# Attention key parts of heads 2 to 7 repeated into partitions 64 to 127 by DMA from SP's queue instead of by ScalarE and VectorE

## The chip, the core and the metric

The kernel runs on one core of a Trainium2 chip. It is written against the engines directly: TensorE (PE), VectorE (DVE), ScalarE (ACT), GpSimd (POOL) and SyncE (SP), each with its own instruction stream, ordered among each other by semaphores only. The metric is the device time of one execution in microseconds (us), as the median of several executions.

## The reference, cut to what matters

A small vision transformer: a token embedding from sines and cosines, one attention block with relative positions and a feed-forward layer, then a second block with a global norm and a mixture of experts. The change lies in the first attention, which for 4 images of 513 tokens, width 192, 8 heads of 64 channels computes

```
q = (h1 @ wq).reshape(b, l, H, DK)
k = (h1 @ wk).reshape(b, l, H, DK)
bias = (qr + uk + vr) * scale
scores = jnp.einsum('bihd,bjhd->bhij', q, k) * scale + bias
attn = jax.nn.softmax(scores, axis=-1)
out = jnp.einsum('bhij,bjhd->bihd', attn, v)
```

## The kernel before, in words

Scores are wanted at more than the precision of one reduced-precision product, so q and k are each held as a first part and a rest. `q` has the first part of a head in partitions 0 to 63 and its rest in partitions 64 to 127. `kh` has the key's first part, `kl` its rest, each of them in both halves of the partitions, so that one product over 128 partitions with `kh` and one with `kl` give all four combinations (`score`, L692).

The products of an image are the list `PRODS` (L512): 13 products n = 0 to 12, two heads to a product. Products 0 to 3 (`EARLY`) are made during the image before, 4 to 12 at the start of the image. Product 3 is the key of heads 0 and 1; 8, 10 and 12 are the keys of heads 2/3, 4/5 and 6/7; 7, 9 and 11 the queries of the same heads. For each, `take` on ACT copies the first part out of PSUM (L811), and `take` on DVE subtracts it from PSUM to get the rest (L937). `repeat` on ACT then copies `kh` from partitions 0 to 63 into 64 to 127 (L820), and `repeat` on DVE does the same for `kl` (L954). ACT's `repeat` of product n stands in its stream after its `take` of product n+1, the last one (product 12) after the exponential of tile 0. DVE's stands right after its own `take`, the last one after tile 2's `add_bias`. PSUM is shared out in four pairs of banks by a list written out by hand (`late_pair`, L518): a product waits until the product that had its pair was taken.

After the products, the image's 40 tiles g (8 heads times 5 tiles of 112 or 65 query rows) go round one loop. On PE each step has `score(g)` (L692), `flip(g-3)` (transposes, L705) and `position(g+10)` (L674), ten tiles ahead. `position_out` copies the position product into the ring `pos` of RT = 4 buffers, by ACT (L832) or, for every second tile from tile 5 on, by DVE (L963); it waits until the transfer that reads the buffer's former content is done. `add_bias` (DVE, L973) makes the scores with their bias and its ring `bias` has MR = 5 buffers. ACT's exponential is L845, DVE's reciprocal L988, POOL's product L616, and `put` copies the transposed probabilities out (ACT L840, DVE L983).

SP issues all DMAs, in this order for each step g: the store of position tile g from `pos` to the DRAM tensor `shear` (L571), then the load of the skewed bias tile g-4 (L582), which waits for its store and for `add_bias` of tile g-9. So SP's program is one list in which each instruction waits for those ahead of it. Position tiles 0 to 9 are made between the products, tile 10 after `score(0)`.

Of the kernel before, what the change touches and what calls it, by code (L numbers as in the profile page):

```python
# [11 lines left out]
F32 = mybir.dt.float32  # L12
# [13 lines left out]
PADL = L + 1  # L26
# [9 lines left out]
H1, DK1, DV1, NPOS = 8, 64, 24, 32  # L36
# [27 lines left out]
def stand_alone(eng, passed):  # L64


    eng.sem_inc(passed, 1)
# [402 lines left out]
def attention_phase(nc, s):  # L470
# [8 lines left out]
    AHEAD = 10  # L479
# [16 lines left out]
    sem = lambda n: s.sem(f"a_{n}")  # L496
# [4 lines left out]
    (pos_done, pos_out_a, pos_out_d, scores_done, biased, exp_done, flipped, put_a, put_d) = (  # L501
        sem("pos_done"), sem("pos_out_a"), sem("pos_out_d"), sem("scores_done"), sem("biased"), sem("exp_done"),
        sem("flipped"), sem("put_a"), sem("put_d"))
    passed, cls_kept = sem("passed"), sem("cls_kept")
    stored, bias_in = [sem(f"stored{i}") for i in range(RING)], [sem(f"bias_in{i}") for i in range(MR)]
    (total_inv, weighed, values_done, values_out, wo_done, image_done, pad_set) = (
        sem("total_inv"), sem("weighed"), sem("values_done"), sem("values_out"), sem("wo_done"), sem("image_done"),
# [4 lines left out]
    PRODS = [("p", 0), ("p", 1), ("q", 0), ("k", 0), ("v", (0, 1)), ("v", (2, 3)), ("v", (4,))] + [  # L512
        (k, p) for p in range(1, H1 // 2) for k in "qk"]
# [6 lines left out]

    after_product = lambda n, w: [g for g in [2 * (n - EARLY) + w - 2] if 0 <= g < AHEAD]
    NP = len(PRODS)
    first_parts = lambda n: sum({"v": 0, "p": 1}.get(kind, 2) for kind, _ in PRODS[:n])
    NHI = first_parts(NP)
    with ExitStack() as ctx:
# [6 lines left out]
        kh, kl = sb("kh", [128, H1, PADL + 2], F32R), sb("kl", [128, H1, PADL + 2], F32R)  # L532
# [15 lines left out]
        @block.sync  # L548
        def _(sp):
            def stack(i, hg):  # L550

                sp.wait_ge(part3, i * 2 + hg + 1)
                for j in range(G4):
                    for part in range(3):
                        sp.dma_start(qpos[NPOS * part:NPOS * part + NPOS, hg * G4 + j, :],
                                     parts[NPOS * j:NPOS * j + NPOS, hg, part, :]).then_inc(stacked[hg], 16)

            def image(b, more):
                for g in range(NG + LAG):
                    if g < NG:  # L560
                        i0, r = TILES[g % NT]
                        x = g % RING

                        if g >= RING:
                            sp.wait_ge(bias_in[(g - RING) % MR], 16 * (b * (NG // MR) + (g - RING) // MR + 1))
                            stand_alone(sp, passed)
                        if by_vector(g):
                            sp.wait_ge(pos_out_d, b * vector_parts(NG) + vector_parts(g + 1))
                        else:
                            sp.wait_ge(pos_out_a, b * scalar_parts(NG) + scalar_parts(g + 1))  # L570
                        sp.dma_start(s.shear[x, 0:r, L - 1 - REACH:L - 1 - REACH + PADL],  # L571
                                     pos[0:r, g % RT, :]).then_inc(stored[x], 16)
                    if g >= LAG:
                        h = g - LAG
                        i0, r = TILES[h % NT]
                        x = h % RING
                        sp.wait_ge(stored[x], 16 * (b * (NG // RING) + h // RING + 1))
                        stand_alone(sp, passed)
                        if h >= MR:
                            sp.wait_ge(biased, b * NG + (h - MR) + 1)  # L580
                        row = s.shear.rearrange("x r c -> x (r c)")[x, L - 1 - i0:L - 1 - i0 + r * (s.PITCH - 1)]
                        sp.dma_start(bias[0:r, h % MR, 0:L],  # L582
                                     row.rearrange("(r c) -> r c", r=r)[:, 0:L]).then_inc(bias_in[h % MR], 16)
                if more:
                    stack(b + 1, 0)
                    stack(b + 1, 1)
                sp.wait_ge(biased, (b + 1) * NG)
                stand_alone(sp, passed)

            stack(0, 0)  # L590
            stack(0, 1)
            with sp.Fori(0, B - 1) as b:
                image(b, True)
            image(B - 1, False)

        @block.gpsimd
# [31 lines left out]
        def _(pe):  # L628
# [20 lines left out]
            def image(b, more):  # L649
# [10 lines left out]
                def position(g):  # L660
                    h, t = divmod(g, NT)
                    i0, r = TILES[t]
                    if g == 0:
                        pe.wait_ge(prod_free, b * NP + EARLY)
                    else:
                        wait_position_out(g)
                    if g == AHEAD:
                        pe.wait_ge(prod_free, b * NP + last_late(NP, 2) + 1)
                    if g == 0:
# [8 lines left out]
                def score(g):  # L678
                    h, t = divmod(g, NT)
                    i0, r = TILES[t]  # L680
                    if g < 2:
                        pe.wait_ge(prod_free, b * NP + last_late(NP, score_pair(g)) + 1)
                    if t == 0:
                        pe.wait_ge(repeated_h, b * H1 + h + 1)
                        pe.wait_ge(repeated_l, b * H1 + h + 1)
                    if last_in_pair[g] is not None:
                        pe.wait_ge(biased, b * NG + last_in_pair[g] + 1)
                    if g == SUMMING[-1] + 2:
                        pe.wait_ge(values_out, b * 4 + 2)
                    for w in range(2):  # L690
                        for k in (kh, kl):
                            mm = pe.matmul(pairs[score_pair(g)][w][0:r, 0:HALF + 1], q[:, h, i0:i0 + r],  # L692
                                           k[:, h, w * HALF:w * HALF + HALF + 1], start=k is kh, stop=k is kl)
                    mm.then_inc(scores_done, 1)

                def flip(g):
                    i0, r = TILES[g % NT]
                    pe.wait_ge(weighed, b * NG + g + 1)
                    if g == 0:
                        pe.wait_ge(prod_free, (b + 1) * NP)  # L700
                    if g >= 1:
# [30 lines left out]
                def late_product(n):  # L732
# [7 lines left out]
                    else:  # L740
                        pe.wait_ge(prod_free, b * NP + last_late(n, late_pair(n)) + 1)

# [16 lines left out]
                for g in range(NG):  # L759
                    score(g)  # L760
                    if g >= LATE:
                        flip(g - LATE)
                    if g + AHEAD < NG:
                        position(g + AHEAD)
                    if g in SUMMING:
                        for n in range(2 * (g - SUMMING[0]), 2 * (g - SUMMING[0]) + 2):
                            values(0, n // NT, n % NT, G4 * NT, SUMMING[0] - 2)
                    for w in range(2):
                        if more and g - w in EARLY_TILES:
                            early_product(EARLY_TILES[g - w], w)  # L770
# [24 lines left out]
        def _(act):  # L795
# [17 lines left out]
            def repeat(i, n):  # L813

                kind, p = PRODS[n]
                if kind == "k":
                    for e in range(2):
                        h = 2 * p + e
                        act.wait_ge(hi_done, i * NHI + first_parts(n) + e + 1)
                        act.copy(kh[DK1:128, h, 0:PADL], kh[0:DK1, h, 0:PADL].bitcast(F32)).then_inc(repeated_h, 1)  # L820
# [5 lines left out]
            def image(b, more):  # L826
# [26 lines left out]
                for n in range(EARLY, NP):  # L853
                    for g in after_product(n, 0):
                        position_out(g)
                    take(b, n, late_pair(n))
                    for g in after_product(n, 1):
                        if not by_vector(g):
                            position_out(g)
                    if n > EARLY:  # L860
                        repeat(b, n - 1)
# [20 lines left out]
                if more:  # L882
                    take(b + 1, LAST_EARLY, 2)
                    repeat(b + 1, LAST_EARLY)
# [19 lines left out]
        def _(dve):  # L904
# [42 lines left out]
            def repeat(i, n):  # L947

                kind, p = PRODS[n]
                if kind == "k":  # L950
                    dve.wait_ge(s.lo_done, i * H1 + 2 * p + 2)
                    for e in range(2):
                        h = 2 * p + e
                        dve.tensor_copy(kl[DK1:128, h, 0:PADL], kl[0:DK1, h, 0:PADL].bitcast(F32)).then_inc(repeated_l, 1)  # L954

            def image(b, more):
# [60 lines left out]
                if more:  # L1017
                    take(b + 1, LAST_EARLY, 2)
                    repeat(b + 1, LAST_EARLY)
# [1234 lines left out]
def program(nc, d):  # L2254
    with ExitStack() as ctx:
# [31 lines left out]
        s.raw_table, s.m_w2 = room(3 * NPOS, PADL), room(128, FF1 // 128, D)  # L2287
        embed_phase(nc, s)
        attention_phase(nc, s)
        free_semaphores()  # L2290
        s.yT = sb("yT", [128, 2, B, PADL])
# [128 lines left out]
```

## Time and profile before

| | us |
|---|---|
| median of 3 runs | 1006.21 |
| their range | 1001.24 to 1008.29 |
| the profiled execution, device time | 1011.46 |
| its span, first to last instruction | 1009.7 |

The profile is of one execution. Busy time of PE, DVE, ACT and POOL is a share of the span; an instruction that only waits or issues a DMA is not busy time. The attention of the four images lies between about 300 and 716 us of the span; the examples below are of the second image, whose products begin near 426 us and whose tile loop runs from 445 to 515 us.

### The profile page before, as it was taken

The page shows a single profiled execution, that of the slowest core. Times are in us where ns is not written, and L with a number is a line of the kernel's source. Part 1 is how long each engine was busy: PE and PEld are TensorE (multiplying, and loading weights), DVE is VectorE, ACT ScalarE, POOL GpSimd, SP SyncE. Part 2 cuts the span into 40 slices and gives each one's busy share as a digit, 9 for nine tenths or more (in the row PEclk, how much of TensorE's full clock was granted, in tenths as well). Part 3 has the DMA queues.
Part 4 walks back from the last instruction along what each step waited for, and adds up shares of the span by engine and source line. Part 5 has one row for each costly group of instructions (what it writes and reads, how often), then busy time and mean ns, then how long its engine had stood idle before and what let it go on. Part 6 is the DMA issues. An engine that isn't in the chain of part 4 may idle for free. (4 is left out here: it accounts for less than half of the span.)

```text
span 1009.7 us, 20063 instructions
## 1 busy us (share of the span) xinstructions
PE 905.0 (90%) x6459; PEld 804.0 (80%) x6459; DVE 730.7 (72%) x1705; ACT 646.9 (64%) x1211; POOL 144.1 (14%) x204
## 2 busy tenths in 40 slices
PE   5999999999987889889988998898699996699996
PEld 5999999999985777667766776776498875599995
DVE  7899979979932786479657964887556334687785
ACT  4766757857724787579757975898444321766862
POOL 1000000000000143214421531144400000000000
PEclk9999999999987899999999999999779998699998
DMA  8003110179912686169616961695400030442201
GB/s 269 22 22 97 38 32 0 36 128 146 138 35 61 178 256 200 43 193 281 192 44 196 286 181 49 202 298 154 106 1 1 17 87 24 122 155 76 91 1 63
DMA packets 83799, 114.06 MB, mean 113 GB/s; under 512 B 12272, under 2 KB 44477, under 8 KB 83725
## 3 DMA queue, kind: packets, MB, share of 16 engines
q1 hardware_dynamic: 82636, 112.39, 41.1%
q10 hardware_dynamic: 1088, 0.79, 0.2%
q8 instruction: 34, 0.56, 0.2%
q14 instruction: 41, 0.33, 0.1%
HBM read 62.31 MB, written 47.67 MB: 109 GB/s over the span
## 5 line engine op out<-in xcount | busy, mean ns | idle before, releaser
L400 PE MATMUL psum<-w,feat 128*128 128x192 f32 x960 | 167.8, 330 | 13.6 <-ACT feat L330 10.1
L400 PEld LDWEIGHTS psum<-w,feat 128*128 128x128 f32 x960 | 156.5, 192 | 14.5 <-issue 10.0
L616 POOL TENSOR_SCALAR a_scores<-a_scores,a_inv 112x514 f32<-112x514 f32 (+1 forms) x160 | 113.0, 707 | 275.5 <-DVE a_inv L988 275.2
L973 DVE CUSTOM_DVE_ANT_0 a_scores<-psum,a_bias 112x514 f32<-112x514 f32 (+1 forms) x160 | 110.0, 688 | 50.1 <-PE psum L692 42.9
L845 ACT ACTIVATE a_scores<-a_scores,a_least 112x514 f32<-112x514 f32 (+1 forms) x160 | 116.7, 729 | 9.6 <-DVE a_least L973 8.3
L705 PE MATMUL psum<-ident,a_scores 112*112 112x112 f32 (+1 forms) x800 | 103.1, 261 | 14.6 <-DVE a_probsT L983 8.9
L418 PE MATMUL psum<-w_parts,parts 128*128 128x384 f32 x368 | 113.9, 374 | 2.5 <-DVE parts L232 2.3
L330 ACT ACTIVATE feat<-turn 128x1024 f32<-128x1024 f32 (+1 forms) x60 | 58.5, 974 | 85.1 <-DVE turn L215 52.4
L705 PEld LDWEIGHTS psum<-ident,a_scores 112*112 112x112 f32 (+1 forms) x800 | 78.1, 137 | 35.6 <-POOL a_scores L616 17.4
L692 PE MATMUL psum<-a_kh,a_q 128*112 128x258 f32 (+1 forms) x320 | 101.9, 339 | 1.0 <-DVE a_least L973 1.0
L420 PE MATMUL psum<-w_parts,parts 128*128 128x192 f32 x384 | 97.3, 253 | 0.0
L840 ACT COPY a_probsT<-psum 112x336 f32<-112x336 f32 (+1 forms) x160 | 66.6, 416 | 34.8 <-PE psum L705 30.4
L643 PE MATMUL psum<-h1T,place 96*128 (+3 forms) x320 | 85.4, 405 | 3.6 <-DVE a_q L937 2.2
L692 PE MATMUL psum<-a_kl,a_q 128*112 128x258 f32 (+1 forms) x320 | 85.8, 288 | 0.0
L674 PE MATMUL psum<-a_table,a_qpos 96*112 96x257 bf16 (+1 forms) x320 | 67.7, 294 | 18.3 <-DVE a_pos L963 7.4
L832 ACT COPY a_pos<-psum 112x514 f32<-112x514 f32 (+1 forms) x88 | 51.9, 589 | 36.2 <-PE psum L674 30.8
L420 PEld LDWEIGHTS psum<-w_parts,parts 128*128 128x128 f32 x384 | 74.2, 193 | 0.0
L418 PEld LDWEIGHTS psum<-w_parts,parts 128*128 128x128 f32 x368 | 69.7, 189 | 3.9 <-issue 3.6
L643 PEld LDWEIGHTS psum<-h1T,place 96*128 96x128 f32 (+1 forms) x320 | 60.0, 201 | 13.6 <-DVE a_q L937 2.9
L215 DVE SCALAR_TENSOR_TENSOR turn<-x,freq,near 128x1024 f32<-128x1024 f32 (+1 forms) x60 | 70.3, 1171 | 0.0
L332 ACT ACTIVATE feat<-near,half_pi 128x1024 f32<-128x1024 f32 (+1 forms) x60 | 63.5, 1059 | 6.8 <-DVE near L221 6.6
L692 PEld LDWEIGHTS psum<-a_kh,a_q 128*112 128x112 f32 (+1 forms) x320 | 55.4, 173 | 11.5 <-issue 8.3
(288 smaller groups left out, 1832.6 us busy)
## 6 DMA issues: line engine op xcount, KB each, us to landing
shear<-a_pos SPq DMA_DIRECT2D x128, 224.9 KB, 3.6
a_bias<-shear SPq DMA_DIRECT2D x128, 224.4 KB, 3.7
shear<-zero SPq DMA_DIRECT2D x20, 448.9 KB, 16.7
e_fc<-in_e_fc_dram SPq DMA_DIRECT2D x16, 384.0 KB, 3.8
x<-in_xT_dram SPq DMA_DIRECT2D x20, 256.0 KB, 3.0
e_proj<-in_e_proj_dram SPq DMA_DIRECT2D x8, 576.0 KB, 5.5
shear<-a_pos SPq DMA_DIRECT2D x32, 130.5 KB
a_bias<-shear SPq DMA_DIRECT2D x32, 130.3 KB
```

Source lines behind the costliest of these rows:

```text
L215: dve.scalar_tensor_tensor(out=turn[:, r, 0:n, :], in0=x[:, c0:c0 + n, :], scalar=freq[:, u:u + 1], in1=near[:, r, 0:n, :], op0=ALU.mult, ...
L400: mm = pe.matmul(sums[m][:, 0:D], feat[:, r, j, 0, 128 * m:128 * m + 128], w[:, k, :], start=begins, stop=ends)
L418: pe.matmul(sums[m][:, 0:2 * D], f(0), w_parts[:, g, j, :, :].rearrange("p a n -> p (a n)"), start=False, stop=False)
L420: mm = pe.matmul(sums[m][:, 0:D], f(1), w_parts[:, g, j, 0, :], start=False, stop=False)
L616: pool.tensor_scalar(row, row, inv[0:TILES[g % NT][1], g % TT:g % TT + 1], 1.0, ALU.mult, ALU.mult).then_inc(weighed, 1)
L643: mm = pe.matmul(out[:, 0:HALF], wt[0:rows, c, 128 * p:128 * p + 128], x, start=c == 0, stop=c == 1)
L674: mm = pe.matmul(pairs[2][w][0:r, 0:HALF], qpos[:, h, i0:i0 + r], table[:, w * HALF:w * HALF + HALF], start=True, stop=True)
L692: mm = pe.matmul(pairs[score_pair(g)][w][0:r, 0:HALF + 1], q[:, h, i0:i0 + r], k[:, h, w * HALF:w * HALF + HALF + 1], start=k is kh, stop= ...
L705: mm = pe.transpose(pairs[3][jb // 3][0:TILE, TILE * (jb % 3):TILE * (jb % 3) + r], scores[0:r, g % TT, TILE * jb:TILE * jb + TILE], s.ide ...
L840: act.copy(probsT[:, slot(g // NT), 0:3, i0:i0 + r], src).then_inc(put_a, 1)
L845: act.activation(scores[0:r, g % TT, 0:PADL], scores[0:r, g % TT, 0:PADL], ACT.Exp, bias=least[0:r, g % TT:g % TT + 1], scale=-1.0, accum_ ...
L973: dve.tensor_tensor_reduce(halves(scores[0:r, g % TT, 0:PADL]), psum2(score_pair(g), r), halves(bias[0:r, g % MR, :]), -1.0 / 8, BIG, ALU. ...
```

## The change

`move_keys` on SP takes the place of both `repeat`s for products 8, 10 and 12. It issues two DMAs, one in `kh` and one in `kl`, each from partitions 0 to 63 to 64 to 127, for two heads at once: 64 partitions times 2 rows of 2056 bytes. They stand in SP's list ahead of the store of position tile 11, 13 and 15. PE's `score` waits for them at the first tile of head 2, 4 and 6 and 3, 5 and 7 (`moved`). For heads 0 and 1 all stays as it was.

```
+    MOVES = {AHEAD + 1: PRODS.index(("k", 1)), AHEAD + 3: PRODS.index(("k", 2)), AHEAD + 5: PRODS.index(("k", 3))}
...
+            def move_keys(b, n):
+                p = PRODS[n][1]
+                for part, ready, count in ((kh, hi_done, b * NHI + first_parts(n) + 2), (kl, s.lo_done, b * H1 + 2 * p + 2)):
+                    sp.wait_ge(ready, count)
+                    stand_alone(sp, passed)
+                    sp.dma_start(part[DK1:128, 2 * p:2 * p + 2, 0:PADL].bitcast(F32), part[0:DK1, 2 * p:2 * p + 2, 0:PADL].bitcast(F32)).then_inc(moved[p], 16)
+
             def image(b, more):
                 for g in range(NG + LAG):
+                    if g in MOVES:
+                        move_keys(b, MOVES[g])
...
                     if t == 0:
-                        pe.wait_ge(repeated_h, b * H1 + h + 1)
-                        pe.wait_ge(repeated_l, b * H1 + h + 1)
+                        if h < 2:
+                            pe.wait_ge(repeated_h, b * 2 + h + 1)
+                            pe.wait_ge(repeated_l, b * 2 + h + 1)
+                        else:
+                            pe.wait_ge(moved[h // 2], b * 32 + 32)
...
             def repeat(i, n):
 
                 kind, p = PRODS[n]
-                if kind == "k":
+                if kind == "k" and p == 0:
```

The last edit is made twice, in ACT's `repeat` and in DVE's.

## Rows read from the trace of the kernel before

**Rows 1.** The page: the span, and the DMA engines' busy tenths in 40 slices

```profile
span 1009.7 us, 20063 instructions
...
DMA  8003110179912686169616961695400030442201
```

**Rows 2.** Windows of the second image: busy us by engine, clock, DMA share, GB/s

```profile
444.00:456.00 12.00, 8.73 (x58) 7.53 (x57) 10.37 (x28) 10.38 (x24) 2.81 (x4) 0.86 0.56 175
456.00:480.00 24.00, 22.20 (x185) 18.58 (x184) 22.34 (x78) 22.38 (x61) 11.93 (x17) 1.00 0.92 283
480.00:520.00 40.00, 37.20 (x340) 28.61 (x339) 26.85 (x85) 29.83 (x73) 15.71 (x21) 1.00 0.50 140
```

**Rows 3.** The two lines of `repeat`: ns min/median/max of one

```profile
L820 ACT CAST a_kh<-a_kh x32: 613/617/622, 313.2 to 646.5; 64x514 fp32r<-64x514 f32 x32
...
L954 DVE CAST a_kl<-a_kl x32: 408/420/630, 314.4 to 648.9; 64x514 fp32r<-64x514 f32 x32
```

**Rows 4.** DVE in order of time, second image: start, us, instruction, idle before

```profile
438.50 0.76 DVE L954 CAST a_kl<-a_kl 64x514 fp32r<-64x514 f32 x2 [0.15 <-DVE a_kl L937]
...
443.01 0.76 DVE L954 CAST a_kl<-a_kl 64x514 fp32r<-64x514 f32 x2 [0.15 <-DVE a_kl L937]
443.80 1.40 DVE L937 TENSOR_TENSOR a_q<-psum,a_q 64x514 fp32r<-64x514 f32 x2
445.23 0.69 DVE L973 CUSTOM_DVE_ANT_0 a_scores<-psum,a_bias 112x514 f32<-112x514 f32 x1
...
448.95 0.67 DVE L973 CUSTOM_DVE_ANT_0 a_scores<-psum,a_bias 112x514 f32<-112x514 f32 x1
...
449.66 0.95 DVE L954 CAST a_kl<-a_kl 64x514 fp32r<-64x514 f32 x2
...
450.73 0.67 DVE L973 CUSTOM_DVE_ANT_0 a_scores<-psum,a_bias 112x514 f32<-112x514 f32 x1
```

**Rows 5.** PE in order of time, the same stretch

```profile
438.46 5.49 PE L643 MATMUL psum<-h1T,place 96*128 x24
...
444.15 0.29 PE L692 MATMUL psum<-a_kl,a_q 128*112 128x258 f32 x1
445.25 0.43 PE L674 MATMUL psum<-a_table,a_qpos 96*112 96x257 bf16 x2 [0.82 <-DVE a_q L937]
...
449.02 0.43 PE L674 MATMUL psum<-a_table,a_qpos 96*112 96x257 bf16 x2 [1.63 <-DVE a_pos L963]
```

**Rows 6.** ACT in order of time, the same stretch

```profile
443.46 1.14 ACT L820 CAST a_kh<-a_kh 64x514 fp32r<-64x514 f32 x2
444.63 1.19 ACT L811 CAST a_kh<-psum 64x514 fp32r<-64x514 f32 x2
```

**Rows 7.** SP's DMA issues: load of bias 10, store of position 15

```profile
455.34 0.31 SPq L582 DMA_DIRECT2D a_bias<-shear  x1
456.25 0.31 SPq L571 DMA_DIRECT2D shear<-a_pos  x1
```

**Rows 8.** The stores (L571) from 455 to 480 us: issue to landing

```profile
DMA to landing us min/median/max: 2.9/4.1/4.7
```

**Rows 9.** DVE's copy of position tile 19, which reuses tile 15's buffer

```profile
461.04 0.68 DVE L963 COPY a_pos<-psum 65x514 f32<-65x514 f32 x1
```

**Rows 10.** Waits from 325 to 740 us: us in total, times, longest

```profile
ACT a_pos L832 <- DMA shear<-a_pos: 4.7, 3, 2.7
```

**Rows 11.** A load to 64 partitions, window 276 to 283 in 40 slices

```profile
GB/s 0 18 18 0 0 0 0 0 0 0 0 0 0 0 0 177 319 35 248 319 284 461 254 88 206 123 29 29 64 6 0 0 0 0 0 0 0 0 0 0
...
x<-in_a_wqT_dram SPq DMA_DIRECT2D x1, 388.0 KB, 4.0
```

**Rows 12.** A store from 128 partitions, window 296 to 300 in 40 slices

```profile
GB/s 0 0 0 0 0 0 0 0 0 0 0 0 31 369 430 461 399 461 369 369 461 399 185 0 82 0 0 0 0 0 0 0 0 0 0 0 0 0 0 0
...
h_kept<-base SPq DMA_DIRECT2D x1, 384.0 KB, 2.3
```

**Rows 13.** SP's issue of the load to 64 partitions, ns

```profile
L164 SPq DMA_DIRECT2D x<-in_a_wqT_dram x1: 534/534/534, 277.4 to 277.4; - x1
```

More of the change, by code:

```diff
@@ L503, in attention_phase @@
         sem("flipped"), sem("put_a"), sem("put_d"))
-    passed, cls_kept = sem("passed"), sem("cls_kept")
+    passed, cls_kept, moved = sem("passed"), sem("cls_kept"), [sem(f"moved{p}") for p in range(H1 // 2)]
     stored, bias_in = [sem(f"stored{i}") for i in range(RING)], [sem(f"bias_in{i}") for i in range(MR)]
@@ L949, in repeat @@
                 kind, p = PRODS[n]
-                if kind == "k":
+                if kind == "k" and p == 0:
                     dve.wait_ge(s.lo_done, i * H1 + 2 * p + 2)
```

## The prediction

> **What bounds the kernel now.** First the page: the span, and the slices of the DMA engines, in which four humps stand for the four images' tile loops, each with a nine in its middle [rows 1]. The window view then splits one image. From 456 to 480 us everything is nearly full at once: of 24 us DVE is busy 22.34, ACT 22.38, PE 22.20, and the DMA engines 0.92 [rows 2]. From 480 us on PE is the fullest (37.20 of 40 us) and the DMA engines have half their time free. In the window before, 444 to 456 us, PE is busy 8.73 of 12 us and the DMA engines 0.56. So the copies stand in or just ahead of the emptiest stretch of PE and of the DMA queue, while their replacement reaches into the fullest of the queue. Whether the change gains is settled between 438 and 462 us of an image. I read that stretch in order of time, DVE first [rows 4], then PE and ACT at the same moments [rows 5, 6], then SP's issues [rows 7].
>
> **What is removed.** Six of the eight copies an image on each of two engines, 24 of 32 over the kernel. One takes 617 ns on ACT and 420 ns on DVE at the median [rows 3], so 24 x 0.617 = 14.8 us of ACT and 24 x 0.42 = 10.1 us of DVE. That is busy time; the path is worth less. On DVE two pairs of copies of 0.76 us lie among the products and one of 0.95 us after tile 2 [rows 4].
>
> The first pair, at 438.50 us, lies beside PE, which makes products 10 to 12 without a gap from 438.46 to 443.95 us [rows 5]. Its removal alone brings DVE to data that is not there yet: nothing, or the part of it that the second pair lets through.
>
> The second pair, 443.01 to 443.80 us, holds up the subtraction for product 11 directly [rows 4]. PE waits 0.82 us for just that subtraction before position tile 10 [rows 5]. With the pair gone it ends some 0.8 us earlier, at about 444.4. Nothing can take more here: score 0's last matmul ends at 444.15 + 0.29 = 444.44 us, and tile 0's `add_bias`, at 445.23 before, can't be earlier. On ACT the copies from 443.46 on delay the first part of product 12 from 443.95 (PE's end) to 444.63 us [rows 6], a delay of 0.7 that goes with it. I carry 0.8 us to tile 2, from 448.95 to about 448.15.
>
> The third pair, at 449.66 us, stands between tile 2 and tile 3 (450.73). Score 3 is made behind position tile 12 on PE, which waited 1.63 us for DVE and began at 449.02 [rows 5]. Moved 0.8 earlier it begins at 448.2, and the two matmul groups behind it (0.9 us by the same order of work at 445.25 less its wait) are done near 449.1; DVE takes tile 3 at about 449.3. The gain at tile 3 is 450.73 - 449.3 = 1.4 us. The bounds: 0.8 if PE gives back the third pair, and 0.76 + 0.76 + 0.95 = 2.5 if all of DVE's copies count. I take 1.4 an image, also for the first one, whose order is the same.
>
> **What is added on SP.** Six DMAs an image, 24 in all. SP's nearest issue of such a shape, 64 partitions, took 534 ns [rows 13] against 0.31 us for a store or a bias load [rows 7]. A pair costs SP 1.1 us. Its waits are met by then: product 12 is taken before tile 1, and the third pair stands after tile 14's store, four steps of the loop later. Behind the pair are queued the store of position 11, 13 or 15 and all later stores and bias loads. Between the issue of bias 10, ending at 455.65, and store 15 at 456.25 SP has 0.6 us free [rows 7], so the pair pushes store 15 by about 1.1 - 0.6 = 0.5, with its waits 0.6 us. PE's new waits cost nothing: head 2 starts at tile 10, about 12 us after its DMA, and heads 4 and 6 ten and twenty tiles later with DMAs only some 7 us later.
>
> **What is added on the DMA engines.** A move is 64 x 2 x 2056 bytes, 257 KB; a pair 514 KB. No DMA of before goes from half the partitions to the other half, so I bound it. A store of 384 KB from 128 partitions kept its stream going for 11 slices of 0.1 us, 1.1 us [rows 12]: 257 KB in 0.7, a pair in 1.4. A load of 388 KB to 64 partitions took 11 slices of 0.175, 1.9 us, and landed in 4.0 against 2.3 [rows 11, 12]: a pair in 2.5. I put no lower end under 1.4 because those packets were alone in the queue.
>
> The Trainium skill has a rule that speaks against this change (SBUF — State Buffer, section "Door 1: The DMA port swizzle"): a range of 64 partitions reaches only half of the memory's DMA ports, for some 218 GB/s at best. By it a pair would take, as an estimate, 2.4 us. The trace's 388 KB load agrees, at about 209 GB/s.
>
> The first pair falls near 448.7 us, the second near 451.8; from 444 to 456 the queue is idle 0.44 x 12 = 5.3 us [rows 2], room for two pairs of 1.4 to 2.5. The third falls near 455.7, where the cover ends. Its place to hurt is the `pos` ring. Store 15 is issued at 456.25 and lands 4.1 us later [rows 7, 8], at 460.35; DVE's copy of position 19 needs that buffer at 461.04 [rows 9]. The slack is 0.7 us. The new delay of store 15 is the issue, 0.6, plus the pair's time less the 1.1 us by which it starts ahead, plus what the second pair left, 0 to 0.4: 0.6 + 0.3 + 0 = 0.9 us with the fast bound, 0.6 + 1.4 + 0.4 = 2.4 with the slow one. Over the slack that is a wait of 0.2 to 1.7 us, and DVE, busy 93% here, can't make it good. I take 1.0, just above the middle, since the slow row is that with 64 partitions. That stores can be late here at all the trace shows: 3 waits of ACT for one, 4.7 us in all, the longest 2.7 [rows 10].
>
> **The sum.** An image gains 1.4 and gives back 1.0, so 0.4; four images 1.6 us. The profiled execution would go from 1011.46 to about 1009.9. It was 5.25 us above the median of the runs shown, so the median would be 1006.21 - 1.6 = 1004.6 us.
>
> **The rivals.** *The cover holds.* The queue drains between the pairs, and the wait at position 19 stays under the slack. Then 1.4 to 2.5 us an image stay, 5.6 to 10. On top, PE may keep its clock: from 444 to 456 us it was granted 0.86 of full speed [rows 2], that is 28% of 12 us, 3.4 us, at the 1.2 GHz level, after PE had been waiting for DVE (0.82, then 1.63 us). At half speed for 3.4 us at most 1.7 us of work are lost, 6.8 in four images, of which shorter waits may give back some. The middle of this rival is 1006.2 - 8 = 998 us; with the clock as well, 990. For it speaks that only one of three pairs meets the full queue; against it, that the slack is only 0.7 us.
>
> *The queue can't drain.* From 456 to 480 us the DMA engines are busy 0.92. If that is their limit and not only their mean, what the third pair adds stays in front of every store and load until 480, and with pairs of 2.5 us a good part of the second does too: 2 x 2.5 - 0.7 = 4.3 us of waits at the `pos` ring, against a gain of 0.8. That is 3.5 us an image slower, 14 in all: 1020 us. It decides from the point where the second pair is not over when the third is issued, four tiles later. [...] Against it speaks the idle time of 5.3 us ahead. A milder form, a slow pair with 1.7 us of wait and a gain of 0.8, gives 4 x 0.9 = 3.6 us: 1010.
>
> *It removes only hidden work.* PE's unbroken products and its tile loop set the pace, the copies fill gaps, and neither cost nor gain is seen: 1006 us.
>
> **How the numbers follow.** Forecast, 1002 to 1008: 0.45. Cover holds: 0.23, with 0.11 under 996. The queue, mild or full: 0.22, with 0.12 over 1016.3. Hidden work: 0.10. The range leaves out the full queue rival and the clock on top of the first: 994 to 1015. About 1% (10 us) is what a measurement of this kernel can tell from no change. Faster by over that 0.12, within it 0.76, slower 0.12.
>
> **What would show it.** In the changed profile L820 and L954 have 8 instructions each. In the second image tile 3's `add_bias` follows tile 2's by about 1.1 us instead of 1.78, and begins 1.4 us earlier counted from product 10's first matmul. The move DMAs occupy the queue 0.7 to 1.25 us each. ACT's or DVE's `position_out` has waits on `shear` of about 1 us once an image, at tile 19; if there are none, the cover holds, and if they come at tiles 17 to 25 in a row, the queue can't drain. The prediction is wrong if PE waits for `moved`, or if the granted clock between tiles 0 and 6 is another.

## The result, and the profile after

The changed kernel takes 1024.84 us in the median of 4 runs (1022.19 to 1030.08), the kernel before 1003.91 (1001.24 to 1008.29) in the 4 beside it: a ratio of 1.0215, with an interval of 1.017 to 1.0259. It is 21 us slower, and outside the forecast range. The profiled executions are 11.65 us apart (1023.11 and 1011.46), since that of before lay 7.55 us above its median and that of after 1.73 below its own.

The page of after, span and DMA slices [rows 1]:

```profile
span 1021.3 us, 20018 instructions
...
DMA  8003110179802796169716972698120021342201
```

The tile loops' humps are wider than before. The windows of its second image, columns as in [rows 2]:

```profile
444.00:456.00 12.00, 9.40 (x57) 8.30 (x56) 9.24 (x24) 8.35 (x19) 2.77 (x4) 0.87 0.51 138
456.00:480.00 24.00, 19.66 (x142) 16.75 (x141) 16.80 (x57) 17.02 (x45) 8.37 (x13) 0.85 0.98 281
480.00:520.00 40.00, 37.04 (x326) 29.22 (x325) 29.54 (x99) 32.41 (x81) 17.81 (x25) 1.00 0.64 188
```

Up to 456 us nothing is lost. From 456 to 480 DVE falls from 22.34 to 16.80 us of work, ACT from 22.38 to 17.02 and PE from 22.20 to 19.66, at a granted clock of 0.85 instead of 1.00, while the DMA engines are at 0.98. They move 281 GB/s, no more than the 283 before: fuller, and no faster. The waits of after from 325 to 740 us (total, times, longest):

```profile
DVE a_pos L976 <- DMA shear<-a_pos: 19.3, 12, 3.3
...
ACT a_pos L845 <- DMA shear<-a_pos: 8.5, 6, 4.0
```

Before, ACT's waits for a store came to 4.7 us [rows 10] and DVE's to 0.7; now they come to 8.5 and 19.3, 27.8 in all. Some of this is no work of the moves: ahead of the first image's tile 0, at 341.75 us, no move has been issued, and yet ACT and DVE wait there for stores: 2.7 us before, 5.2 after and 11.2 in `e1_neither`, which has no moves. From 340 us on the waits are 2.6 us before, 22.6 after and 2.1 in `e1_neither`. DVE in order of time, the second image:

```profile
447.11 0.69 DVE L986 CUSTOM_DVE_ANT_0 a_scores<-psum,a_bias 112x514 f32<-112x514 f32 x1 [0.47 <-PE psum L705]
...
450.83 0.68 DVE L986 CUSTOM_DVE_ANT_0 a_scores<-psum,a_bias 112x514 f32<-112x514 f32 x1
...
452.04 0.69 DVE L986 CUSTOM_DVE_ANT_0 a_scores<-psum,a_bias 112x514 f32<-112x514 f32 x1 [0.45 <-PE psum L705]
...
457.62 0.69 DVE L976 COPY a_pos<-psum 112x514 f32<-112x514 f32 x1 [0.41 <-DMA shear<-a_pos]
...
463.69 0.69 DVE L976 COPY a_pos<-psum 112x514 f32<-112x514 f32 x1 [3.27 <-DMA shear<-a_pos]
...
468.60 0.69 DVE L976 COPY a_pos<-psum 65x514 f32<-65x514 f32 x1 [1.26 <-DMA shear<-a_pos]
```

The first three are `add_bias` of tiles 0, 2 and 3, the other three the copies of position tiles 15, 17 and 19. PE's product 10 begins at

```profile
440.84 5.49 PE L653 MATMUL psum<-h1T,place 96*128 x24
```

so tile 3 follows it by 11.20 us, against 450.73 - 438.46 = 12.27 before [rows 4, 5]: the gain is there, 1.07 us. Then DVE stands still for 3.27 us at tile 17. PE in turn waits for that copy:

```profile
464.44 0.68 PE L684 MATMUL psum<-a_table,a_qpos 96*112 96x257 bf16 x2 [2.85 <-DVE a_pos L976]
```

SP in order of time shows what DVE waits for:

```profile
450.77 0.68 SPq L564 DMA_DIRECT2D a_kh<-a_kh  x1
451.66 0.62 SPq L564 DMA_DIRECT2D a_kl<-a_kl  x1
452.41 0.69 SPq L581 DMA_DIRECT2D shear<-a_pos  x1
453.30 1.43 SPq L592 DMA_DIRECT2D a_bias<-shear  x1
...
455.93 0.60 SPq L564 DMA_DIRECT2D a_kh<-a_kh  x1
456.70 0.60 SPq L564 DMA_DIRECT2D a_kl<-a_kl  x1
457.41 1.01 SPq L581 DMA_DIRECT2D shear<-a_pos  x1
458.61 1.54 SPq L592 DMA_DIRECT2D a_bias<-shear  x1
...
461.24 0.60 SPq L564 DMA_DIRECT2D a_kh<-a_kh  x1
462.02 0.60 SPq L564 DMA_DIRECT2D a_kl<-a_kl  x1
462.73 0.56 SPq L581 DMA_DIRECT2D shear<-a_pos  x1
```

A pair takes 1.48 us of SP's list (455.93 to 457.41). The store and the load issued right behind it take 1.01 and 1.54 us to issue, where 0.31 was usual [rows 7]. The store of 457.41 is that of position 13, and by its own view

```profile
DMA to landing us min/median/max: 6.2/6.2/6.2
```

it lands at 463.6, where DVE's 3.27 us end. Before, store 13 was issued at 452.33 and landed 3.6 us later, 2.3 us ahead of the copy of position 17 at 458.23. Counted from product 10 it is now issued 2.7 us later and takes 2.6 us longer to land. The queue behind the pairs, from 450 to 466 us in slices of 0.4 us, and the moves with their size and time to landing:

```profile
GB/s 370 82 10 72 287 267 206 216 221 201 206 134 185 216 252 293 267 211 221 247 344 349 154 170 159 180 201 231 267 262 339 339 344 339 236 164 221 170 190 216
...
a_kh<-a_kh SPq DMA_DIRECT2D x3, 257.0 KB, 5.2
a_kl<-a_kl SPq DMA_DIRECT2D x3, 257.0 KB, 5.8
```

Three times the rate falls to between 134 and 221 GB/s for 2 us or more: for 8 slices from 452.4 us, for 5 from 458.8, and for 5 from 464.0 to the window's end (it is at 247 and more from 466.0 on). Each time that begins 1.6 to 2.9 us after a pair's first issue and lasts 2.0 to 3.2 us; in between the rate reaches 349. The DMA engines are busy 0.8 or more in these slices.

### The profile page after: what moved, and what is told of

Its sections match the earlier page's. It is cut to its first block and busy times, and to the rows that moved or that the text cites. A ratio compares the mean times of both kernels' runs of the same rounds, so it can differ in the third digit from the quotient of the medians.

```text
span 1021.3 us, 20018 instructions
## 1 busy us (share of the span) xinstructions
PE 904.1 (89%) x6459; PEld 802.4 (79%) x6459; DVE 720.4 (71%) x1681; ACT 633.8 (62%) x1187; POOL 141.5 (14%) x204
## 5 line engine op out<-in xcount | busy, mean ns | idle before, releaser
L718 PEld LDWEIGHTS psum<-ident,a_scores 112*112 112x112 f32 (+1 forms) x800 | 81.0, 139 | 32.9 <-POOL a_scores L626 15.3
L705 PE MATMUL psum<-a_kh,a_q 128*112 128x258 f32 (+1 forms) x320 | 105.4, 348 | 1.0 <-DVE a_least L986 1.0
L684 PE MATMUL psum<-a_table,a_qpos 96*112 96x257 bf16 (+1 forms) x320 | 69.8, 302 | 31.0 <-DVE a_pos L976 21.5
L705 PE MATMUL psum<-a_kl,a_q 128*112 128x258 f32 (+1 forms) x320 | 88.3, 295 | 0.0
L976 DVE COPY a_pos<-psum 112x514 f32<-112x514 f32 (+1 forms) x72 | 49.4, 687 | 39.6 <-PE psum L684 20.1
L684 PEld LDWEIGHTS psum<-a_table,a_qpos 96*112 96x112 bf16 (+1 forms) x320 | 33.7, 134 | 48.6 <-DVE a_pos L976 29.4
```

Source lines behind the costliest of these rows:

```text
L684: mm = pe.matmul(pairs[2][w][0:r, 0:HALF], qpos[:, h, i0:i0 + r], table[:, w * HALF:w * HALF + HALF], start=True, stop=True)
L718: mm = pe.transpose(pairs[3][jb // 3][0:TILE, TILE * (jb % 3):TILE * (jb % 3) + r], scores[0:r, g % TT, TILE * jb:TILE * jb + TILE], s.ide ...
```

## The experiments

Each kernel is the changed one with the edit shown; the ratio is to the kernel before, and a period is the time from one image's first `add_bias` to the next image's, three of them in a trace. For the changed kernel they come from

```profile
341.75 0.69 DVE L986 CUSTOM_DVE_ANT_0 a_scores<-psum,a_bias 112x514 f32<-112x514 f32 x1 [0.47 <-PE psum L705]
...
656.14 0.69 DVE L986 CUSTOM_DVE_ANT_0 a_scores<-psum,a_bias 112x514 f32<-112x514 f32 x1 [0.33 <-PE psum L705]
```

and sum to 314.4 us; before it was 644.05 - 342.64 = 301.4. The periods are of one execution and scatter by some us, so the ratios carry the verdicts where both exist: the traced execution of before took 7.55 us more than the median, that of e4_tiny (1015.09 us) was the slowest of its ten, that of e7_early_late (997.09) the fastest.

| kernel | moves | ratio [interval] | three periods, us |
|---|---|---|---|
| before | copies | 1 | 301.4 |
| after | SP, 64 to 64 partitions | 1.0215 [1.017, 1.0259] | 314.4 |
| e1_neither | none | 1.0013 [0.9975, 1.0051] | 297.4 |
| e16_neither_again | none | 0.9965 [0.9937, 0.9994] | 294.6 |
| e4_tiny | SP, rows of 64 bytes | 1.0053 [1.0017, 1.0089] | 307.0 |
| e3_wide | SP, 128 to 128 | 1.0144 [1.0061, 1.0227] | 307.6 |
| e11_pool_tiny | GpSimd, 64 bytes | one run, 1000.56 us | 298.9 |
| e12_pool_wide | GpSimd, 128 to 128 | one run, 1020.08 us | 306.3 |
| e8_pool | GpSimd, 64 to 64 | 1.0225 [1.0156, 1.0293] | 317.8 |
| e5_ring8 | as after, 8 `pos` buffers | 1.0201 [1.0138, 1.0265] | 312.3 |
| e10_single | SP, one DMA a step | 1.0237 [1.0166, 1.0309] | 312.3 |
| e6_early | SP, after the stores of tiles 9 and 10 | 0.9983 [0.9948, 1.0018] | 296.8 |
| e7_early_late | two early, third at step 34 | 0.9983 [0.9946, 1.002] | 295.0 |
| e13_second | e7 with the second at its place | 1.0037 [1.0001, 1.0073] | 302.2 |
| e14_third | e6 with the third at its place | 1.0037 [1.0006, 1.0068] | 303.8 |
| e9_act | ScalarE, where its copies stood | 0.9952 [0.9922, 0.9982] | 295.3 |
| e15_act_again | the same | 0.9961 [0.9932, 0.999] | 297.2 |

**The gain side alone.** No copies for heads 2 to 7, no moves:

```
-                    if g in MOVES:
-                        move_keys(b, MOVES[g])
...
-                        else:
-                            pe.wait_ge(moved[h // 2], b * 32 + 32)
...
-                                           k[:, h, w * HALF:w * HALF + HALF + 1], start=k is kh, stop=k is kl)
+                                           k[:, h % 2, w * HALF:w * HALF + HALF + 1], start=k is kh, stop=k is kl)
```

> The copies of heads 2 to 7 are left out on ScalarE and VectorE and no DMA takes their place; the scores of all heads read the keys of heads 0 and 1. It gives the worth of the removal alone. My sum had 1.4 us an image: 5.6 us, about 0.994 of the kernel before. If the copies only fill gaps, 1.000. If the removal itself disturbs the order (the same slowness as the changed kernel without any DMA), 1.02.

1.0013, with periods 4.0 us shorter in three images, 1.3 an image. The interval holds no change and leaves out the 0.56% expected, so it was measured again at the end:

> The kernel of e1 once more. By its three image periods (297.4 against 301.4) it should be 5 us faster than before, 0.995; its first timing gave 1.001 with an interval of 0.998 to 1.005. It should not be faster than e15 if ScalarE's issues cost nothing, the keys being read from other heads being the only other difference.

0.9965, some 3.5 us. The two timings together give 0.998, give or take 0.002: some 2 us, less than the 5.6 forecast, and from these two alone not clear of nothing. With the two timings of `e9_act` below (0.9952 and 0.9961), which also has no copies, the gain is clear of noise; its size lies between 2 and 5 us. What the moves cost is then 2.0 to 2.5% (1.0215 against 1.0013 and 0.9965), 5 to 6 us an image.

**What of a move costs: its issue, its bytes or its form.** The rows cut to 64 bytes (scores read the keys as in the kernel without moves):

```
-... part[DK1:128, 2 * p:2 * p + 2, 0:PADL].bitcast(F32), part[0:DK1, 2 * p:2 * p + 2, 0:PADL].bitcast(F32)
+... part[DK1:128, 2 * p:2 * p + 2, 0:16].bitcast(F32), part[0:DK1, 2 * p:2 * p + 2, 0:16].bitcast(F32)
```

> As the changed kernel, the same six DMAs an image between the same halves with the same 128 rows, but of 64 bytes each instead of 2056 (the scores read the keys of heads 0 and 1). Theories A and B, the time of the data: near the kernel without any move, 0.995 to 1.000 of the kernel before, no wait for a store above 1 us. Theory C, the issue of 0.6 us and the number of rows: 1.01 to 1.02.

SP of this kernel in order of time:

```profile
455.82 0.60 SPq L564 DMA_DIRECT2D a_kh<-a_kh  x1
456.59 0.60 SPq L564 DMA_DIRECT2D a_kl<-a_kl  x1
457.30 0.53 SPq L581 DMA_DIRECT2D shear<-a_pos  x1
458.02 0.31 SPq L592 DMA_DIRECT2D a_bias<-shear  x1
458.48 0.33 SPq L581 DMA_DIRECT2D shear<-a_pos  x1
459.01 0.30 SPq L592 DMA_DIRECT2D a_bias<-shear  x1
459.56 0.31 SPq L581 DMA_DIRECT2D shear<-a_pos  x1
```

Next to no data, and the issue still takes 0.60 us. Behind it SP issues back to back, with 0.2 us between two: a store and a load take it 1.0 us (two tiles from 457.30 to 459.56 with the first store's longer issue), and a tile takes DVE 1.4 us in this stretch (17 `add_bias` of before begin between 456.2 and 479.0), so by this estimate it wins back 0.4 us a tile, and a pair's 1.5 us stay in its list for four tiles, while the next pair stands two tiles behind it. The kernel is slower by 0.4 to 0.9% of the time (1.0053 against the two without moves), 1 to 2 us an image. The same bytes, rows and order of issues, from 128 partitions to 128 (the third pair also waits until the first has landed, whose tiles it overwrites; keys of heads 6 and 7 share the slots of heads 2 and 3):

```
-                    sp.dma_start(part[DK1:128, 2 * p:2 * p + 2, 0:PADL].bitcast(F32), part[0:DK1, 2 * p:2 * p + 2, 0:PADL].bitcast(F32)).then_inc(moved[p], 16)
+                    sp.dma_start(part[:, 6 + (p == 2), 0:PADL].bitcast(F32), q[:, 0, 0:PADL].bitcast(F32)).then_inc(moved[p], 16)
```

> As the changed kernel, the same six DMAs an image at the same places with the same bytes (257 KB) and the same 128 rows of 2056 bytes, but from 128 partitions to 128 partitions (query tile of head 0 into unused key tiles; the scores read the keys of heads 0 and 1). Theory A, a DMA between halves of the partitions runs at about half the rate (the packets of the pairs took 0.15 to 0.2 us instead of 0.085): a pair takes 1.4 us instead of 3, the waits at the pos ring mostly go, 1.000 to 1.006 of the kernel before. Theory B, the bytes are too many for the queue whatever their shape: stays at 1.02. Theory C, SyncE's issue and the queue's handling of a DMA: stays at 1.015 to 1.02.

Its queue from 450 to 466 us, the same slices as above:

```profile
GB/s 370 360 221 216 283 344 375 257 257 252 344 303 247 334 308 308 313 313 308 267 226 349 293 267 278 334 339 380 385 308 329 323 370 303 287 375 360 313 334 313
...
a_kh<-a_q SPq DMA_DIRECT2D x2, 257.0 KB, 4.1
a_kl<-a_q SPq DMA_DIRECT2D x2, 257.0 KB, 4.7
```

The three stretches near 200 GB/s are gone, but for a few single slices. The windows of after and of this kernel for the same 16 us, columns as in [rows 2]:

```profile
450.00:466.00 16.00, 11.43 (x74) 9.99 (x75) 9.89 (x34) 10.10 (x25) 5.25 (x8) 0.81 0.92 226
```

```profile
450.00:466.00 16.00, 13.31 (x99) 11.39 (x96) 11.20 (x37) 12.21 (x32) 5.60 (x8) 0.89 1.00 311
```

The ratio is 1.0144 against 1.0215. The intervals overlap, so that the form makes the moves dearer is likely but not shown by the times; the periods say the same from both queues (307.6 against 314.4 from SP, 306.3 against 317.8 from GpSimd). Most of the loss stays, so the form is not needed for one. That a half-range has a lower ceiling is the rule weighed ahead (the Trainium skill, SBUF — State Buffer, "Door 1: The DMA port swizzle", some 218 GB/s). The slices under the moves, 134 to 221 GB/s, agree, though stores and loads are moved in them too.

**Off SP's queue, on GpSimd's.** After GpSimd's tiles 0, 2 and 4, in the full form, then with the 64 bytes and the 128 partitions of above:

```
+                    if g in (0, 2, 4):
+                        n = MOVES[AHEAD + 1 + g]
...
+                            pool.wait_ge(ready, count)
+                            stand_alone(pool, passed)
+                            pool.dma_start(part[DK1:128, 2 * p:2 * p + 2, 0:PADL].bitcast(F32), part[0:DK1, 2 * p:2 * p + 2, 0:PADL].bitcast(F32)).then_inc(moved[p], 16)
```

> The same six DMAs, same shape and bytes, from GpSimd's queue after its tiles 0, 2 and 4, so SyncE's list is as before. Theory C (issue on SyncE's list) says: the share of the loss that the 64-byte moves showed, some 3 us an image, goes; what stays is the time of the data between the halves, about 2 us an image: 1.005 to 1.01. If the loss is the data alone, in whatever queue, 1.015 to 1.02. A third way: GpSimd needs several us for the descriptors and its products for the transposes come late: above 1.02.

> As e8 (GpSimd's queue) with the 64-byte rows of e4. By the image period in the trace (tile 0 to tile 0, three of them): 297.4 us with no DMA, 307.0 with 64-byte rows from SyncE, 317.8 with full rows from GpSimd. If SyncE's issue was the whole cost of the tiny ones, 297 to 299 here. If the 128 rows cost time in the DMA engines themselves, 305 to 308. If GpSimd's own time for issuing makes its products late, also above 302, and then its waiters show it.

> As e8 with the DMAs of e3: same bytes and rows, 128 partitions to 128. Three image periods: if the data at the full rate fit into the queue and only the half-partition rate is dear, 299 to 304; if bytes as such end on the path, 308 to 314, near e8's 317.8.

Without data the moves are now nearly free: the one execution, 1000.56 us, lies below all ten of e4_tiny (1005.83 to 1015.09), its period at 298.9 against 297.4 without moves. With 128 partitions they cost what they cost from SP (306.3 against 307.6), and in the full form as well (1.0225 against 1.0215). So issues in SP's list alone and data in the full queue alone are each enough for a loss. No sum of the two is seen, though the intervals (up to 0.7% to each side) would hide the 0.4 to 0.9% of the list. With full moves from GpSimd SP's list is held up all the same: in the second image seven of its stores and loads in a row took 0.5 to 1.9 us each to issue. Taking the issues off SP did not help at this place. The waits of the full form:

```profile
DVE a_pos L981 <- DMA shear<-a_pos: 20.8, 10, 4.8
...
ACT a_pos L850 <- DMA shear<-a_pos: 10.7, 6, 4.6
```

**A deeper ring.** If the loss were the reuse of four buffers, eight would end it (keys kept in six slots to make room, and the third pair waits until the first has landed):

```
-    RT, MR, TT = 4, 5, LATE + 1
+    RT, MR, TT = 8, 5, LATE + 1
```

> As the changed kernel, moves at their old places, but the ring of position tiles has 8 buffers instead of 4 (room for it comes from key tiles that this kernel doesn't use: the scores read the keys of heads 0 and 1, heads 6 and 7 share the slots of heads 2 and 3). If the loss passes through late stores of a ring of four, the waits for stores go: 0.995 to 1.003 of the kernel before, even with SyncE's list and the queue as full as before. If it passes through the bias loads or the clock, it stays above 1.01.

1.0201. No wait for a store is left; instead there is one that the changed kernel hasn't:

```profile
DVE a_scores L990 <- DMA a_bias<-shear: 10.5, 8, 2.6
```

The bias tiles come late instead. The `pos` ring is where the lateness showed, and four buffers are not its cause.

**Spreading.** One DMA a step, the pairs at steps 11/12, 16/17 and 25/26, so that SP may catch up in between:

```
-    MOVES = {AHEAD + 1: PRODS.index(("k", 1)), AHEAD + 3: PRODS.index(("k", 2)), AHEAD + 5: PRODS.index(("k", 3))}
+    MOVES = {AHEAD + 1: PRODS.index(("k", 1)), AHEAD + 6: PRODS.index(("k", 2)), AHEAD + 15: PRODS.index(("k", 3))}
```

> The changed kernel with its six DMAs spread in SyncE's list: one a step instead of two, and the pairs at steps 11, 16 and 25 (each split over two steps) instead of 11, 13 and 15. If the loss comes from the heap (three pairs within five steps), most of it goes: 1.000 to 1.006. If from 456 to 480 us of an image every DMA more ends on the path, because the queue and SyncE's list are both nearly full there, it stays at 1.012 to 1.02.

1.0237: no help. DVE's and ACT's waits for stores come to 43.1 us, and from 340 us on to 30.7 against the 22.6 of the changed kernel. Steps 16, 17, 25 and 26 all lie in the full stretch, in which before issues the stores of tiles 15 to 31.

**Place.** The moves between a step's store and its load, outside the full stretch:

```
-    MOVES = {AHEAD + 1: PRODS.index(("k", 1)), AHEAD + 3: PRODS.index(("k", 2)), AHEAD + 5: PRODS.index(("k", 3))}
+    MOVES = {}
+    BETWEEN = {AHEAD - 1: (PRODS.index(("k", 1)), PRODS.index(("k", 2))), AHEAD: (PRODS.index(("k", 3)),)}
...
+                    for n in BETWEEN.get(g, ()):
+                        move_keys(b, n)
```

> The changed kernel with other places: the pairs of heads 2/3 and 4/5 after the store of position tile 9 and the pair of heads 6/7 ahead of the store of tile 10, where the DMA engines are mostly idle. If the loss is one of place (the data of pairs two and three in front of the stores of the pos ring), the waits at tiles 17 and 19 go and it is 0.995 to 1.005 of the kernel before. If the pairs cost wherever they stand, 1.015 to 1.02. The third pair now waits for the keys of heads 6/7, which can hold up store 10 by about 1 us; with a ring of four that is still ahead of tile 14.

The edit puts the third pair behind the store of tile 10 (a step's `BETWEEN` follows its store), not ahead of it as the expectation says, so it doesn't hold up that store.

In e7_early_late the third pair stands at `AHEAD + 24` instead, behind the full stretch:

> First two pairs early as in e6, the third at SyncE's step 34, where the DMA engines have half their time free; head 6 starts at tile 30. If the place of the third pair in e6 (in front of store 10, waiting for the keys of heads 6/7) still costs, this is 1 to 3 us faster than e6; if not, the same within 2 us. 0.990 to 1.002.

Both 0.9983, what the kernel without moves gives in its two timings together: the whole loss is gone, with the same bytes, form, issues and queue. Then one pair at its old place, the others out of the way. e13_second has the first pair at `AHEAD - 1`, the second in `MOVES` at `AHEAD + 3`, the third at `AHEAD + 24`; e14_third has the first two at `AHEAD - 1` and the third at `AHEAD + 5`.

> Only the second pair stands at its old place, ahead of store 13; the first is early (behind store 9) and the third late (step 34), both of which cost nothing in e7. My prediction had room for this pair (queue idle 5.3 us around it) and only a wait at the third. If that holds alone, 0.995 to 1.001 like e7. If the second pair meets a full list by itself, 1 to 3 us an image more than e7: 1.003 to 1.01.

> Only the third pair stands at its old place, ahead of store 15; the first two are early. It is the pair at which the prediction put its whole cost, 1.0 us an image (0.2 to 1.7). The second pair alone cost 2.4 us an image more than none (three image periods 302.2 against 295.0). If the third alone is like it, three periods of 300 to 303; if my 1.0 was right for it, 298.

Each costs 0.54% (1.0037 against 0.9983), 1.35 us an image; the traces say 2.4 (302.2 - 295.0, over three) and 2.3 (303.8 - 296.8). The intervals reach 0.3 to 0.4% to each side, so the size is rough and only its sign is fairly clear. All three pairs cost 2.3% against the early ones, 5.8 us an image. By the times that is more than three lone pairs would (4.1); by the traces, 5.9 against 2.4 and 2.3, the first pair would have to cost 1.2 for a plain sum. No run has the first pair alone at its place, so that a pair costs more when the list and the queue are still behind from the last one is likely and not shown. Where the waits fall is plain. DVE in order of time, e13_second's copy of position 17, then e14_third's of position 19:

```profile
455.94 0.69 DVE L979 COPY a_pos<-psum 112x514 f32<-112x514 f32 x1 [2.44 <-DMA shear<-a_pos]
```

```profile
461.93 0.69 DVE L979 COPY a_pos<-psum 65x514 f32<-65x514 f32 x1 [1.28 <-DMA shear<-a_pos]
```

**From ScalarE's queue.** Where `repeat` stood on ACT, and no longer in SP's list:

```
-                if kind == "k" and p == 0:
+                if kind == "k" and p:
+                    for part, ready, count in ((kh, hi_done, i * NHI + first_parts(n) + 2), (kl, s.lo_done, i * H1 + 2 * p + 2)):
+                        act.wait_ge(ready, count)
+                        stand_alone(act, passed)
+                        act.dma_start(part[DK1:128, 2 * p:2 * p + 2, 0:PADL].bitcast(F32), part[0:DK1, 2 * p:2 * p + 2, 0:PADL].bitcast(F32)).then_inc(moved[p], 16)
+                elif kind == "k":
```

> The same six DMAs from ScalarE's queue, where its copies stood, so the first two pairs run among the products and SyncE's list is as before. If ScalarE's issue costs no more than SyncE's (0.6 us a DMA, 1.2 a pair, against 1.14 for its two copies), ScalarE is as busy as before, and with the DMA engines free there the time is that of the early placement, 0.995 to 1.002. If a queue of its own still delays the stores through the shared DMA engines, 1.005 to 1.01.

> The kernel of e9 once more, beside the one without copies and moves, to see whether removing the copies is worth anything in time. By the three image periods (295.3 against 301.4 before) it should be 6.1 x 4/3 = 8 us faster, 0.992; if 0.998 or above, the periods promise what the device time doesn't hold.

0.9952 and 0.9961: this version beats both kernels, by 4 to 5 us over before, and equals the one without any moves. The window just ahead of its second image's full stretch (tile 0 at 441.26 us), and an issue on ACT:

```profile
439.00:451.00 12.00, 9.62 (x61) 8.41 (x60) 9.09 (x26) 8.35 (x20) 2.78 (x4) 0.86 1.00 273
```

```profile
438.94 0.60 ACTq L831 DMA_DIRECT2D a_kh<-a_kh  x1
```

The DMA engines are at 1.00 in a stretch that they had half free before [rows 2]. The moves are done when the loop needs the queue.

## Why the prediction was wrong, step by step

**Where to look** was right for the gain (438 to 452 us) and too short for the loss: DVE still waits for a store at 468.60 us.

**The removed copies** were sized somewhat high: 1.4 us an image forecast, 1.07 measured at tile 3, and 2 to 5 us in the whole kernel instead of 5.6. The second pair gave 0.5 us at tiles 0 and 2 instead of 0.8 (tile 0 follows product 10 by 6.27 us, before by 6.77). L833 and L967 (L820 and L954 before) have 8 instructions each. Tile 3 follows tile 2 by 1.21 us (forecast 1.1).

**"A pair costs SP 1.1 us"** was near (1.48 with the gaps). What failed is the next sentence, "SP has 0.6 us free": one gap ahead of store 15 was taken for the slack of the list. In the loop the list is some 70% full, a pair takes four tiles to win back, and another stands two tiles behind it. So a delay passes on: counted from product 10, which began 2.4 us later here, the pairs were forecast at 448.7, 451.8 and 455.7 and issued at 448.4, 453.6 and 458.9. The slip of 1.8, then 3.2 us, put the second pair half and the third wholly into the full stretch. By the 64-byte rows the list alone costs 1 to 2 us an image: there store 13 was issued 1.4 us later than before, against 2.7 with the data.

**"Room for two pairs of 1.4 to 2.5"** failed. The idle 5.3 us are a mean over 444 to 456 us; the pairs don't begin until 450.77, 448.4 on the clock of before, and stores and loads want that time too. The windows of before, split there:

```profile
444.00:448.40 4.40, 2.25 (x16) 1.58 (x14) 3.92 (x9) 4.22 (x10) 0.00 (x0) 1.00 0.29 98
448.40:456.00 7.60, 6.49 (x42) 5.95 (x43) 6.45 (x20) 6.16 (x15) 2.81 (x4) 0.78 0.72 219
```

From 448.4 on the queue is idle 0.28 x 7.6 = 2.1 us, room for one pair. The second pair alone costs 1.35 us an image where it stood, and was costed at nothing. The rate of the whole queue was down for 2.0 to 3.2 us a pair, with stores and loads in it, against bounds of 1.4 and 2.5 for the pair by itself. The slow bound came from the right row, the one with 64 partitions, but was used for the wait at one tile only. That its 209 GB/s agree with the rule of 218 says little: slices in it reach 319 and 461 GB/s, and a load of 64 KB is moved in the same window.

**The third pair, 1.0 us an image,** is not far from what it costs alone (1.35 by the times, 2.3 by the trace; the bounds were 0.2 and 1.7), and alone it makes DVE wait at tile 19 as forecast (1.28 us in e14_third). Part of that is luck: the slack of 0.7 us took the stretch's median of 4.1 us for store 15, which by its own view landed in 2.9, so the slack was 1.9. The term that was mis-sized is the cost of the moves, 1.0 us an image for one pair instead of 5 to 6 us for all three. Store 15 was forecast to land 0.9 to 2.4 us later; counted from product 10 it was issued 4.1 us later and took 5.8 us to land, 7.0 later in all. The wait came two tiles sooner (tile 17, 3.27 us) and again at 19 (1.26).

**The rivals.** "The queue can't drain" had the mechanism, nearly the place (it had waits at tiles 17 to 25; they came at 15 to 19) and two thirds of the size: 14 us slower against 21. It was given 0.22, and 0.12 in its full form, because the idle time ahead of 456 us spoke against it. Its deciding point, whether the second pair is over when the third is issued, was right: the second pair's last DMA landed at 462.8 us, the third's first was issued at 461.24. It could have been worked out from SP's rows: a pair's 1.1 us, by the prediction's own figure, against two tiles' 0.8 of slack. It named the DMA queue alone; e4_tiny shows that SP's list does it too. Another queue for the moves does not help: from GpSimd's they delay the stores as much. "The cover holds" is what happens with the moves placed early (e9_act), at 4 to 5 us of gain rather than 8.

**The clock** between tiles 0 and 6 was as before (0.87 against 0.86), so the larger rival's extra 8 us were not to be had. PE did not wait for `moved`. The clock fell to 0.85 from 456 to 480 us instead. Behind PE's wait of 2.85 us for DVE, from 464.4 to 467.6 us, it was granted 0.50, which is the 1.2 GHz level. That probably adds to the loss, but no kernel here takes it out by itself, and its share stays open. The wait of 3.27 us comes about equally from late issue and slow landing: store 13's 2.7 and 2.6 us, less its slack of 2.3, make 3.0.

## What to carry to other kernels

A DMA that replaces a cheap copy is paid for in the queue and in the issuing engine's list, and the price depends on when: these moves cost nothing that could be measured before or after the full stretch of the queue, and 5 to 6 us an image just ahead of it and inside it. Before moving work to DMA, divide the issue time of a loop's DMAs by the loop's period: with 1.0 of 1.4 us used, a delay of 1.5 us lasts some four tiles, and a second one inside those four falls into the same backlog. A mean share of idle time over a window is no room if the new transfers begin in its second half: here 5.3 us of it became 2.1.

## What was unexpected in the hardware

- The issue of a DMA took 0.60 us with 64 partitions and two rows each, whether its rows were 2056 or 64 bytes long, from SP and from ACT alike, against 0.30 for a store of 112 rows: its cost is in its form, not its bytes.
- Behind such a pair the next store and load took 0.6 to 1.5 us each to issue instead of 0.3 when the moves carried their data, and 0.3 to 0.5 when they had 64-byte rows. With the full moves on GpSimd's queue SP's issues took up to 1.9 us in the second image. So data in a backed-up queue also holds up the engine that issues, whichever engine issued them. The Trainium skill (DMA: Bandwidth & Descriptors, "Issuing engines are not separate DMA queues") calls the time that issuing from several engines saves "usually small relative to the DMA itself"; here it was 1 to 2 us an image in the kernel with the tiny moves, and nothing to be seen in the one with full ones.
- Moves between the two halves of the partitions brought the whole queue down to 134 to 221 GB/s for 2.0 to 3.2 us a pair, with the stores and loads that were in it. The same bytes between 128 partitions left it at 311 GB/s in the mean.
